# Gram product in two row halves behind bank 6, three accumulators on VectorE, and high parts of the split pair chunks made by GpSimd

## The reference, cut to what matters

```python
def _cin_layer(X0, Xi, W, b):           # X0 (512,39,16), Xi (512,Fi,16), W (128, 39*Fi)
    Wr = W.reshape(H, F0_, Fi)
    return jnp.einsum('hjk,bjd,bkd->bhd', Wr, X0, Xi) + b[None, :, None]
# three layers of 128 channels; each layer's output is summed over d and feeds
# a dense tower 400 -> 512 -> 256 -> 1 together with a 16-wide context
```

## Time and profile before

| | us |
|---|---|
| three runs, median | 657.04 |
| lowest, highest | 656.72, 657.56 |
| profiled execution, first to last instruction (its span; no other time is on record for it) | 664.5 |
| TensorE busy in it | 633.7 (95%) |
| VectorE, ScalarE, GpSimd busy | 561.9, 557.3, 443.1 |
| mean granted TensorE clock | 0.995 |

### The profile page before, as it was taken

How to read it: one execution, slowest core, us unless ns; L and a number is a source line. 1 busy time by engine, 2 the same in 40 slices (tenths; PEclk the granted TensorE clock), 3 DMA queues, 4 the chain that set the end, 5 groups by cost and what they waited for, 6 DMA issues and landing times.

```text
span 664.5 us, 11375 instructions
## 1 busy us (share of the span) xinstructions
PE 633.7 (95%) x2616; PEld 477.0 (72%) x2616; DVE 561.9 (85%) x878; ACT 557.3 (84%) x1940; POOL 443.1 (67%) x504
## 2 busy tenths in 40 slices
PE   2689999999999999999999999999999999989998
PEld 2656767777777777777777777777777777767874
DVE  3538788889899898989898989898989989899890
ACT  2348788989898999999998999998989998999773
POOL 7555897777777778687777787777777535152700
PEclk9799999999999999999999999999999999999999
DMA  8245533242424233242423333323242320200000
GB/s 292 22 61 105 162 38 87 51 87 56 84 56 80 59 58 84 40 102 33 90 41 84 57 86 55 87 52 81 57 85 55 67 68 6 69 27 0 1 0 1
DMA packets 91117, 43.58 MB, mean 66 GB/s; under 512 B 80630, under 2 KB 83780, under 8 KB 88943
## 3 DMA queue, kind: packets, MB, share of 16 engines
q1 hardware_dynamic: 84058, 41.77, 28.1%
q0 software_dynamic: 5120, 1.29, 2.2%
q10 hardware_dynamic: 1904, 0.15, 0.2%
HBM read 36.39 MB, written 1.81 MB: 57 GB/s over the span
## 4 chain that ended last, share of the span: by engine, by line
PE 75%; DVE 8%; ACT 7%; issue 6%; DMA 3%; DVEq 1%; POOL 0%; SPq 0%; another core or an unknown queue 0%
PE yb L1128 16%; PE yb L1124 16%; PE yb L1125 16%; PE p L1089 10%; PE pq L1101 6%; ACT yb L765 5%; DVE x L941 3%; DVE acc L935 3%; DMA gram<-in_L_rec_W_dram 2%; PE yb L1026 2%; DMA emb<-in_table_dram,idx 1%; DVE x1l L896 1%; PE yb L1237 1%; PE p L1182 1%; PE p L1214 1%
## 5 line engine op out<-in xcount | busy, mean ns | idle before, releaser
L765 ACT ACTIVATE yb<-yb,x0t 128x128 f32<-128x128 f32 x1728 | 467.2, 391 | 56.0 <-PE yb L1128 49.6
L935 DVE TENSOR_TENSOR acc<-acc,yb 128x512 f32<-128x512 f32 (+1 forms) x512 | 323.4, 674 | 33.8 <-ACT yb L765 30.9
L1124 PE MATMUL yb<-w1h,x1h 128*128 128x512 f32 (+1 forms) x640 | 293.8, 459 | 5.0 <-DVE acc L935 3.8
L1128 PE MATMUL yb<-w1h,x1l 128*128 128x512 f32 (+1 forms) x640 | 247.4, 387 | 0.0
L1125 PE MATMUL yb<-w1l,x1h 128*128 128x512 f32 (+1 forms) x640 | 247.1, 386 | 0.0
L497 POOL DMA_INDIRECT emb<-in_table_dram,idx x160 | 153.0, 956 | 53.1 <-issue 44.4
L1124 PEld LDWEIGHTS yb<-w1h,x1h 128*128 128x128 f32 x640 | 120.1, 188 | 59.4 <-DVE acc L935 25.3
L1125 PEld LDWEIGHTS yb<-w1l,x1h 128*128 128x128 f32 x640 | 120.5, 188 | 39.6 <-issue 18.0
L1128 PEld LDWEIGHTS yb<-w1h,x1l 128*128 128x128 f32 x640 | 120.1, 188 | 24.8 <-DVE x1l L896 0.4
L568 POOL TENSOR_TENSOR late<-late,x0r 117x512 f32<-117x512 f32 (+1 forms) x105 | 132.7, 1298 | 4.6 <-DMA late<-x_scratch 4.3
L544 POOL TENSOR_TENSOR bdiag<-mask,x0t 128x312 f32<-128x312 f32 x64 | 45.7, 714 | 107.0 <-PE pq L1101 106.4
(11 more groups left out here) (124 smaller groups left out, 377.2 us busy)
## 6 DMA issues: line engine op xcount, KB each, us to landing
late<-x_scratch SPq DMA_DIRECT2D x45, 312.0 KB
late<-x_scratch SPq DMA_DIRECT2D x30, 234.0 KB
x0r<-x_scratch SPq DMA_DIRECT2D x15, 234.0 KB
emb<-in_table_dram,idx POOLq DMA_INDIRECT x160
gram<-in_L_rec_W_dram SPq DMA_DIRECT2D x1, 2496.0 KB
late<-x_scratch SPq DMA_DIRECT2D x15, 156.0 KB
spare<-spare SPq DMA_DIRECT2D x28, 78.0 KB
x_scratch<-emb SPq DMA_DIRECT2D x75, 20.0 KB
```

The costliest lines, as they stand in the source:

```text
L765: op = act.activation(part, part, ACT.Copy, scale=x0t[u][:, t, j:j + 1])
L935: dve.tensor_tensor(part, part, parts(y_bank(t, m), n), ALU.add).then_inc(summed, 1)
L1124: pe.matmul(y[:, 0:w], hi, w1h[:, at:at + w], start=True, stop=False)
L1128: pe.matmul(y[:, 0:w], lo, w1h[:, at:at + w], start=False, stop=True).then_inc(bank_ready, 1)
```

## The change

The gram becomes two matmuls. Each takes 64 of the 128 rows (four samples) of `x2` and of a `bdiag` that is now half as wide (4 samples x 40 columns), and writes 160 columns: the first half into the last 160 columns of VectorE's second buffer, the second half into the first 160 columns of `pq`, which lies next to it. It is issued behind bank 6 instead of bank 3 and waits also until VectorE has scaled bank 3 of the running tile. `y_bank` no longer alternates: banks 0 and 6 share one buffer, bank 3 has the other. Bank 0 now waits for the scale of bank 6 one tile back, bank 3 for the copy of the gram three tiles back.

VectorE scales all three of its banks into accumulator columns of their own; `acc` grows from 9 to 13 columns, the sum of bank 6 falls away and the fold reads 13 columns. The three multiplies of GpSimd and the copy of ScalarE change places: ScalarE's `high_pairs` goes, and GpSimd multiplies each split chunk twice, once into an fp32r tile (the high part) and once in place. Further: the mask is folded to half width in the prologue by one GpSimd addition, `x0a` and `x0t3` move into the memory of `gram`, and the five slots of W2's transposes move by some banks.

```diff
+HALF_B = TILE_B // 2
+HALF_P = P // 2
+HALF_GRAM = HALF_B * GRAM
...
-N_ACC = 2
-BEGINS = DVE_BANKS[0:N_ACC]
+N_ACC = N_DVE
 PARTS = N_ACC * BANK_F + 1
 
 
 DVE_ORDER = (("sum before", 8), ("scale", 0), ("sum before", 9), ("scale", 3), ("sum", 1), ("sum", 2),
-             ("sum", 4), ("fold before", 0), ("scale", 6), ("sum", 5), ("sum", 7), ("sum", 6))
+             ("sum", 4), ("fold before", 0), ("scale", 6), ("sum", 5), ("sum", 7))
 SEAM_ORDER = tuple(x for x in DVE_ORDER if x[0] != "fold before") + (("fold before", 0),)
-SUM_ORDER = (1, 2, 4, 5, 7, 6, 8, 9)
+SUM_ORDER = (1, 2, 4, 5, 7, 8, 9)
+ACC_OF = {0: 0, 3: 1, 6: 2, 1: 0, 2: 1, 4: 0, 5: 2, 7: 1, 8: 0, 9: 2}
 N_SUM = len(SUM_ORDER)
-GRAM_AT = 3
-GRAM_COPY_AT = 4
+GRAM_AT = 6
+GRAM_COPY_AT = 7
...
-W2_SLOTS = ((4, 6), (4, 9), (5, 6), (5, 9), (6, 9))
+W2_SLOTS = ((4, 2), (4, 9), (5, 2), (5, 9), (6, 2))
...
-        bdiag = [sb(f"bdiag{u}", [P, TILE_B, GRAM]) for u in range(2)]
+        bdiag = [sb(f"bdiag{u}", [P, HALF_B, GRAM]) for u in range(2)]
...
+        x0t3 = flat[:, 15360:15360 + TILES * ROWS].rearrange("p (t r) -> p t r", t=TILES)
+        x0a = flat[:, 15872:15872 + TILES * COLS].rearrange("p (t j) -> p t j", t=TILES)
...
+        two = pb("two", 2)
+        pq = two[:, 512:1024]
+        yb = [pb(f"yb{i}") for i in range(ACT_RING)] + [pb("yd0"), two[:, 0:512]]
         ya, yd = yb[0:ACT_RING], yb[ACT_RING:RING]
         p0 = pb("p0")
-        pq = pb("pq")
+        gram_out = two[:, 512 - HALF_GRAM:512 + HALF_GRAM]
...
-            return yd[(t * N_DVE + DVE_BANKS.index(m)) % DVE_RING]
+            return yd[DVE_BANKS.index(m) % DVE_RING]
...
+            pool.tensor_tensor(mask[:, :], mask8[:, 0:HALF_B], mask8[:, HALF_B:TILE_B], ALU.add).then_inc(consts, 1)
+            pool.wait_ge(consts, 6)
...
-                                   mask[:, :, None].to_broadcast([P, TILE_B, FIELDS]),
-                                   x0t[u][:, t, None, 0:FIELDS].to_broadcast([P, TILE_B, FIELDS]),
+                                   mask[:, :, None].to_broadcast([P, HALF_B, FIELDS]),
+                                   x0t[u][:, t, None, 0:FIELDS].to_broadcast([P, HALF_B, FIELDS]),
                                    ALU.mult).then_inc(bdiag_ready, 1)
...
+                if c in SPLIT and at_least(g, FIRST_SPLIT):
+                    pool.tensor_tensor(pair_h[SPLIT.index(c)][0:rows, :], pairs[0:rows, c, :], x0r[0:rows, :],
+                                       ALU.mult).then_inc(pair_high, 1)
+                    pool.wait_ge(pair_high, highs(g, c))
                 pool.tensor_tensor(pairs[0:rows, c, :], pairs[0:rows, c, :], x0r[0:rows, :],
                                    ALU.mult).then_inc(pairs_ready, 1)
...
-                if c in ACT_SPLIT:
-                    pool.wait_ge(pair_high, highs(g, c))
-                else:
-                    pool.wait_ge(pairs_ready, g * CHUNKS + c + 1)
-                    pool.tensor_copy(h[0:rows, :], pairs[0:rows, c, :]).then_inc(pair_high_by_pool, 1)
-                    pool.wait_ge(pair_high_by_pool, highs(g, c))
+                pool.wait_ge(pairs_ready, g * CHUNKS + c + 1)
                 pool.tensor_tensor(l[0:rows, :], pairs[0:rows, c, :], h[0:rows, :].bitcast(F32),
                                    ALU.subtract).then_inc(pair_low, 1)
...
-            def high_pairs(g, c):
-
-                rows = ROWS if c < CHUNKS - 1 else LAST_ROWS
-                act.wait_ge(pairs_ready, g * CHUNKS + c + 1)
-                act.activation(pair_h[SPLIT.index(c)][0:rows, :], pairs[0:rows, c, :], ACT.Copy).then_inc(pair_high, 1)
...
-                if m in BEGINS:
-                    if m == BEGINS[0] and at_least(T, 2):
-                        dve.wait_ge(x2_ready, T - 1)
-                    at = BANK_F * BEGINS.index(m)
-                    dve.tensor_tensor(acc[t % 2][:, :, at:at + BANK_F], parts(y, BANK_F),
-                                      x0t[u][:, t, None, BANK_F * m:BANK_F * (m + 1)].to_broadcast([P, HID, BANK_F]),
-                                      ALU.mult).then_inc(dve_scaled, 1)
-                    return
-                y = y[:, :].rearrange("p (j h) -> p j h", h=HID)
-                dve.tensor_tensor(y, y, x0t[u][:, t, BANK_F * m:BANK_F * (m + 1), None].to_broadcast([P, BANK_F, HID]),
+                if m == DVE_BANKS[0] and at_least(T, 2):
+                    dve.wait_ge(x2_ready, T - 1)
+                at = BANK_F * ACC_OF[m]
+                dve.tensor_tensor(acc[t % 2][:, :, at:at + BANK_F], parts(y_bank(t, m), BANK_F),
+                                  x0t[u][:, t, None, BANK_F * m:BANK_F * (m + 1)].to_broadcast([P, HID, BANK_F]),
                                   ALU.mult).then_inc(dve_scaled, 1)
 
             def add_bank(T, t, m):
                 n = fields_of(m)
-                k = SUM_ORDER.index(m)
-                if k < N_ACC:
-                    dve.wait_ge(dve_scaled, T * N_DVE + k + 1)
+                earlier = [x for x in SUM_ORDER[0:SUM_ORDER.index(m)] if ACC_OF[x] == ACC_OF[m]]
+                if earlier:
+                    dve.wait_ge(summed, sums_by(T, earlier[-1]))
                 else:
-                    dve.wait_ge(summed, sums_by(T, m) - N_ACC)
-                if m in ACT_BANKS:
-                    dve.wait_ge(act_scaled, T * N_ACT + ACT_BANKS.index(m) + 1)
-                else:
-                    dve.wait_ge(dve_scaled, T * N_DVE + DVE_BANKS.index(m) + 1)
-                at = BANK_F * (k % N_ACC)
+                    dve.wait_ge(dve_scaled, T * N_DVE + ACC_OF[m] + 1)
+                dve.wait_ge(act_scaled, T * N_ACT + ACT_BANKS.index(m) + 1)
+                at = BANK_F * ACC_OF[m]
                 part
...
-            def gram_product(T, p):
+            def gram_product(T, p, own=None):
+
                 pe.wait_ge(x2_ready, T + 1)
                 pe.wait_ge(bdiag_ready, T + 1)
                 if at_least(T, 1):
                     pe.wait_ge(gram_copied, T)
-                pe.matmul(pq[:, 0:TILE_B * GRAM], x2[p][:, :], bdiag[p][:, :, :].rearrange("p b c -> p (b c)"),
-                          start=True, stop=True).then_inc(gram_done, 1)
+                pe.wait_ge(dve_scaled, (T + 2 if own is None else own) * N_DVE + 2)
+                for h in range(2):
+                    rows = slice(h * HALF_P, (h + 1) * HALF_P)
+                    op = pe.matmul(gram_out[:, h * HALF_GRAM:(h + 1) * HALF_GRAM], x2[p][rows, :],
+                                   bdiag[p][rows, :, :].rearrange("p b c -> p (b c)"), start=True, stop=True)
+                op.then_inc(gram_done, 1)
...
-                of, ring = (ACT_BANKS, ACT_RING) if m in ACT_BANKS else (DVE_BANKS, DVE_RING)
-                k = of.index(m)
-                if k >= ring:
-                    bank_free(T, of[k - ring])
-                elif at_least(T, 1):
-                    bank_free(T - 1, of[k - ring])
+                if m == DVE_BANKS[0]:
+                    if at_least(T, 1):
+                        bank_free(T - 1, DVE_BANKS[2])
+                elif m == DVE_BANKS[1]:
+                    if at_least(T, 3):
+                        pe.wait_ge(gram_copied, T - 2)
+                    elif at_least(T, 1):
+                        bank_free(T - 1, m)
+                elif m == DVE_BANKS[2]:
+                    bank_free(T, DVE_BANKS[0])
+                else:
+                    k = ACT_BANKS.index(m)
+                    if k >= ACT_RING:
+                        bank_free(T, ACT_BANKS[k - ACT_RING])
+                    elif at_least(T, 1):
+                        bank_free(T - 1, ACT_BANKS[k - ACT_RING])
...
-            gram_product(NT - 2, 0)
+            gram_product(NT - 2, 0, NT - 1)
```

More of the change, by code:

```diff
@@ L124, in sb, with pb @@
             return ctx.enter_context(nc.sbuf_tensor(name, shape, dt))
-        def pb(name):
-            return ctx.enter_context(nc.psum_tensor(name, [P, 512], F32))
+        def pb(name, banks=1):
+            return ctx.enter_context(nc.psum_tensor(name, [P, 512 * banks], F32))
         def sem(name):
@@ L133, in tower @@
         ident = sb("ident", [P, P])
-        mask = sb("mask", [P, TILE_B])
+        mask8 = sb("mask8", [P, TILE_B])
+        mask = sb("mask", [P, HALF_B])
         ids_all = sb("ids_all", [P, GROUPS, PER_Q], I32)
@@ L294, in y_bank @@
                 return ya[(t * N_ACT + ACT_BANKS.index(m)) % ACT_RING]
-            return yd[(t * N_DVE + DVE_BANKS.index(m)) % DVE_RING]
+            return yd[DVE_BANKS.index(m) % DVE_RING]
         def sums_by(T, m):
             return T * N_SUM + SUM_ORDER.index(m) + 1
-        ACT_SPLIT = tuple(c for c in SPLIT if c in ACT_HIGH)
-        POOL_SPLIT = tuple(c for c in SPLIT if c not in ACT_HIGH)
         def highs(g, c):
-            by = ACT_SPLIT if c in ACT_SPLIT else POOL_SPLIT
-            return (g - FIRST_SPLIT) * len(by) + by.index(c) + 1
+            return (g - FIRST_SPLIT) * len(SPLIT) + SPLIT.index(c) + 1
         def lows(g, c):
@@ L501, in _ @@
```

(16 more changed lines are left out.)

20 lines of the change are left out of this document (7 added, 13 removed).

## The result

The changed kernel takes 669.32 us (median of 4 runs, 668.44 to 670.11), the kernel before 657.30 beside it: ratio 1.0185, interval 1.0171 to 1.0199. The forecast was 649.5 us; the change made it slower by 12 us. The profiled execution spans 667.5 us.

A forecast was written before the change was run, and what follows sets the result against it. The prediction took TensorE's own stream to set the time, except at the seam between groups. It summed 657.04 - 8.0 (gram) + 0.5 (first groups) = 649.5 us, with a range of 640 to 674.

The forecast's parts named there:

- the cost of the gram: On TensorE: four half passes take 0.41 us instead of 0.54, saving 0.13 a gram, 8.0 us over 62 grams.
- The overlap: Gram halves on TensorE run together: middle passes only, 0.41 us, chance 0.50; wholly, 0.27 us, chance 0.05.
- Rival (3): TensorE's array empties between whole and half rows: +0.19 to +0.37 us a gram, 669 to 680 us; chance 0.21.
- The place and the seam: Gram behind bank 6, at the change between groups: no difference, +0.0 with +-7 us over 15 seams.
- the two ends: Bounds of TensorE's loss per seam: 1.23 us, 0.48 more than now, or 0.29 us, 0.46 less.
- The late signal of 0.94 us: Gathers delay VectorE's scale of bank 3 in a group's last tile by 0.94 us; moving them removes this.
- Its sum, +1.1 to +2.5 us a group: GpSimd's queue: two more multiplies, +2.5 us, and shorter spreads, up to -1.4 us per group; hidden.
- The 2.6 us to spare for chunk 6: SyncE's second copy of chunk 6 starts 2.6 us before TensorE wants it, so it is hidden at nothing.
- The fold's added 0.56: VectorE's fold grows from 9 to 13 columns, taking 0.56 us more per tile.
- The saving of one sum: On VectorE the sum of bank 6 goes, -0.60 us per tile; with the longer fold -0.04 us.
- VectorE is off the path except at the seam: VectorE's change of -0.04 us per tile does not affect the time except at the change between groups.
- the foretold 1.3 us a group: ScalarE loses 28 high parts, 18.4 us in all, 1.3 per group; worth nothing unless ScalarE becomes the bound.

The follow-up runs named there:

- e2: Changed kernel with each pair of half gram matmuls issued twice, result unchanged: 682.91 us in one run.
- e9: Kernel before with a small dummy fp32 matmul of 64 rows, 32 columns directly ahead of each whole gram: 686.32 us in one run.
- e10: Kernel before with a small dummy fp32 matmul of 128 rows, 32 columns directly ahead of each whole gram: 670.18 us in one run.
- e7: Changed kernel with the gram whole again (128 rows, 320 columns) behind bank 6 and ScalarE making the high parts again: 667.74 us, ratio 1.0165.
- c0: Kernel before, run again unchanged: 656.26 us in its one run.
- e16: Kernel before with its whole gram moved behind bank 6, its copy behind bank 7 and W2's slots moved beside them: 666.57 us, ratio 1.0144.
- e6: Changed kernel with ScalarE making the two high parts again, the rest unchanged: 668.42 us, ratio 1.0174.
- e11: Changed kernel with the gram whole behind bank 3, ScalarE's high parts and the alternating bank ring of before, three accumulators kept: 662.74 us, ratio 1.0089.
- e13: e11 with the sums of banks 5 and 7 changed over between accumulators: 658.69 us, ratio 1.0025 to the kernel before.
- e14: Changed kernel with the sums of banks 5 and 7 changed over between accumulators: 669.15 us, ratio 1.0177.
- e15: Kernel before with its fold lengthened from 9 to 13 columns by four of zeros, small tiles and bias moved for room: 668.84 us, ratio 1.0184.
- e4: Kernel before with GpSimd instead of ScalarE making the high parts, nothing else: 656.23 us, ratio 0.9987.
- e12: Changed kernel with VectorE's scale of bank 6 ahead of the fold in three of four tiles: 667.98 us, ratio 1.0163.

## Why the prediction was wrong

**The step that failed is the cost of the gram.** "I take 0.41, a saving of 0.13 us" measured 0.67, a loss of 0.13. The overlap is better than the step assumed, 0.27 of streaming instead of 0.41: the passes of the two halves are interleaved as a pair in each round, though the kernel issues one half after the other. What it priced at nothing is the way into half the rows and back, 0.40 us a gram. e2 shows that this is paid per trip and not per pass, e9 against e10 that the rows alone bring 0.26 of it in another arrangement, and e7's last groups against those of the changed kernel that the halves cost TensorE 0.49 us a group of four grams. Over 62 grams that is 8 us more in the place of 8 us less: 16 of the 19.8 us between forecast and result.

Rival (3) was the mechanism. Its price for both ways, 0.32 to 0.50, holds the measured 0.40, and both its parts are there: the wait for the end (0.09 and 0.10 where it had 0.16) and the load that can't run ahead (0.11 where it had 0.09). Only its sum rested on 0.41 of streaming, so that with 0.27 it alone gives 657 + 8 = 665 and not 669 to 680. That the measured time lies at the edge of that span is chance: the other steps brought it there. The Trainium skill, "TensorEngine Tiling (Array Packing)", Key Properties, says that a change of the tiling mode drains TensorE: the trace agrees, with 0.09 us between the full stream's end and the first half load and 0.10 between the last round's end and the next full load. That every load on the other side of a change is late too is the larger half. I gave this rival 0.21, for want of a row, while the overlap, which had no row either, got 0.55: two sides of one unknown, weighed differently.

**The place and the seam.** No wait of the gram for the fold shows at a seam, the scale of bank 3 in the last tile (290.19) starts as soon as TensorE has done the bank, and bank 4 is late behind the sum of bank 8, all as said. TensorE's timeline in the changed kernel at the seam:

```profile
297.80 0.39 PE L1123 MATMUL two<-w1h,x1l 128*128 128x512 f32 x1
298.51 0.50 PE L1119 MATMUL yb<-w1h,x1h 128*128 128x512 f32 x1 [0.32 <-DVE acc L918]
...
299.31 1.02 PE L1069 MATMUL p<-late,w0t 117*128 117x512 f32 x2
```

and VectorE's:

```profile
290.19 0.69 DVE L904 TENSOR_TENSOR acc<-two,x0t 128x512 f32<-128x512 f32 x1 [0.41 <-PE two L1123]
...
293.30 0.68 DVE L904 TENSOR_TENSOR acc<-yd,x0t 128x512 f32<-128x512 f32 x1
294.11 0.69 DVE L918 TENSOR_TENSOR acc<-acc,yb 128x512 f32<-128x512 f32 x1
295.37 0.69 DVE L918 TENSOR_TENSOR acc<-acc,yb 128x512 f32<-128x512 f32 x1 [0.57 <-ACT yb L760]
295.98 1.88 DVE L924 TENSOR_REDUCE x<-acc 128x128 f32<-128x1664 f32 x1
297.77 0.68 DVE L918 TENSOR_TENSOR acc<-acc,yb 128x512 f32<-128x512 f32 x1
```

From bank 0 at 295.25 to the chunk at 299.31 five banks take 4.06 us, 0.66 lost where before lost 0.75: the step's middle of no difference was right. But that was luck, for neither of the two ends between which it lay held. The late signal of 0.94 us before bank 3's scale belonged to the one execution shown. In the unchanged run c0, which issues the same gathers, that scale starts as TensorE has done the bank, in VectorE's timeline:

```profile
284.10 0.69 DVE L914 TENSOR_TENSOR acc<-yb,x0t 128x512 f32<-128x512 f32 x1 [0.39 <-PE yb L1128]
```

and its seam, in TensorE's timeline from bank 0 to the chunk, loses 4.60 - 3.94 = 0.66 us all the same:

```profile
288.87 0.40 PE L1124 MATMUL yb<-w1h,x1h 128*128 128x512 f32 x1
...
293.47 1.02 PE L1089 MATMUL p<-late,w0t 117*128 117x512 f32 x2
```

So the gathers are not shown to delay VectorE. With the signal on time the step's own working gave a loss of 0.29, not 0.66; one wait that it doesn't have is VectorE's for a bank that ScalarE scales (0.57 us, at 295.37).

What the step left out altogether is that the place sets when GpSimd works. In e16 the place costs 9 us, most of it by that way, while the changed kernel pays 1 to 2 for GpSimd's lateness: its spreads are 0.26 us shorter, and with halves (e6) the copies come in time where with the whole gram (e7) they don't. The edits don't add up: the halves cost TensorE 8 us and spare most of GpSimd's lateness.

**GpSimd.** Its sum, +1.1 to +2.5 us a group, measured +1.5 (26.95 to 28.45); a spread takes 0.45. The 2.6 us to spare for chunk 6 were not there. SyncE issues the copy 6.9 us ahead of the next group's bank 0 (at 295.25), as foretold (291.4 against 298.10, 6.7); its timeline in the changed kernel:

```profile
288.31 0.77 SPq L396 DMA_DIRECT2D spare<-spare  x1
```

But it has to land, and TensorE, whose loads wait for it 3.9 us in all, goes on 2.4 us after the issue, in its timeline:

```profile
290.74 0.50 PE L1059 MATMUL p<-spare,ctx_wide 117*128 117x512 f32 x1
```

The wait of those loads:

```profile
PEld p L1059 <- DMA spare<-spare: 3.9, 11, 0.7
```

The step compared the issue with the use and left out what lies between; before, 5.5 us lay there. In e6, without those waits, the 12 later groups are 1.6 us shorter and the whole 0.9.

**VectorE.** The fold's added 0.56 measured 0.53 (start to start 1.79, 295.98 to 297.77, against 1.26). The saving of one sum was read as -0.60, but a sum now stands directly behind the scale that begins its accumulator (293.30, then 294.11, 0.81 and not 0.60): +0.13 a tile instead of -0.04. With the gram behind bank 3 this decides 4.0 of the 5.5 us that three accumulators cost (e11, e13); in the changed kernel removing it gives nothing (e14). The step's claim that VectorE is off the path except at the seam stands in e15: of four folds, 2.1 us longer a group, TensorE loses 0.62, and 0.54 of it at the seam.

**ScalarE** worked out: 1.2 of the foretold 1.3 us a group gone, worth nothing (e6 puts them back and is no slower; in e4, where only they move, the time stays).

**What stays open.** Of the result, 8 us are the halves and 1 to 2 us GpSimd's late copies. The order of scale 6 and fold is worth 1.3 us (e12); how the 1 to 2 us left share out between the first groups, VectorE's chain at the end and the place (0.17 a group in e16) was not taken apart. The halves were never run alone behind bank 3: their price is read from the changed kernel's own stream and from e7, whose gram differs from e6's in nothing but the halves and the wider spread. Why a load across the change can't run ahead is not shown, only that it doesn't.

## What to carry to other kernels

Price the way into a new mode of the array before the saving inside it: a short matmul on half the rows between full ones paid 0.40 us for the trip and won 0.27, so one pair alone loses. Two pairs in a row took 0.94 us in e2, less than two whole grams at 0.54 each; no run made a kernel of that. Moving a product moves everything that waits for it: the cheap edit "behind bank 6 instead of 3" cost 9 us through an engine with 8 us of slack a group, since slack on average is not slack at a deadline. For a transfer, compare landing with use, not issue with use; where a sum is put matters, not only how many there are; and before a gap in one execution is given a cause and a price, see whether an unchanged run has it.

## What the runs showed of the hardware

- Two fp32 matmuls on different halves of the rows start 7 ns apart in each of their two passes, so the pair streams 0.27 us where one after the other would take 0.54. The Trainium skill, "TensorE: Matmul & The Clock Gate", Part 3, has about 4 ns between starts: close.
- From 128 rows to 64 and back costs 0.40 us around a pair of halves (0.67 less 0.27), once for one pair and for two (0.94 less 0.54).
- An addition on VectorE into the accumulator that the instruction just ahead writes, and for which it waits by a semaphore, starts 0.20 us later than one into another (0.80 against 0.60).
